# Two attention hops on a graph: the near gather from three bf16 parts of the table instead of fp32, with other buffers moved into the table's memory

## What is computed

```
h = concat(emb[head], emb[tail]) @ fc_w.T + fc_b
e = leaky_relu(sum(h * rel_e, -1), 0.2)
w = segment_softmax(e, head)
agg = segment_sum(emb[tail] * w[:, None], head) + emb
emb = agg / max(norm(agg), 1e-12)
```

## Time and profile before

| | |
|---|---|
| median of 3 runs | 5189.71 us |
| the profiled execution | 5187.74 us |
| its span, first to last instruction | 5185.9 us |
| TensorE clock granted, mean of the span | 0.899 |
| instructions | 194597 |
| busy share: PE, PEld, DVE, ACT, POOL | 79%, 64%, 71%, 45%, 62% |

### The profile page before, as it was taken

How to read it: one execution, slowest core, us unless ns; L and a number is a source line. 1 busy time by engine, 2 the same in 40 slices (tenths; PEclk the granted TensorE clock), 3 DMA queues, 4 the chain that set the end, 5 groups by cost and what they waited for, 6 DMA issues and landing times. The chain is left out here.

```text
span 5185.9 us, 194597 instructions
## 1 busy us (share of the span) xinstructions
PE 4116.0 (79%) x51067; PEld 3327.7 (64%) x51068; DVE 3702.4 (71%) x11149; ACT 2328.1 (45%) x5659; POOL 3224.1 (62%) x3241
## 2 busy tenths in 40 slices
PE   2666666629999999999759999999999478888874
PEld 0001111119999999999759999999999356666664
DVE  7988488647777777777767777777777545555555
ACT  6201000016666666666536666666666112222221
POOL 0055677637777777777447777777777067777774
PEclk7667888759999999999879999999999589899897
DMA  7999999936556666566356565665566133333332
GB/s 269 421 410 411 419 419 417 410 86 165 157 160 159 160 159 160 159 159 158 78 142 162 156 161 159 162 158 160 157 161 153 21 68 68 69 69 69 69 69 47
DMA packets 502232, 935.41 MB, mean 180 GB/s; under 512 B 153045, under 2 KB 301966, under 8 KB 452978
## 3 DMA queue, kind: packets, MB, share of 16 engines
q1 hardware_dynamic: 397729, 759.23, 45.5%
q0 software_dynamic: 103328, 174.55, 14.2%
q10 hardware_dynamic: 1072, 0.31, 0.0%
HBM read 917.50 MB, written 14.15 MB: 180 GB/s over the span
## 5 line engine op out<-in xcount | busy, mean ns | idle before, releaser
L1525 POOL DMA_INDIRECT rows<-tab_d,stage_idx x2040 | 1963.0, 962 | 922.7 <-issue 380.1
L1593 PE MATMUL ps_g<-rows,prob 128*128 128x65 f32 x6528 | 867.0, 276 | 188.8 <-issue 148.1
L1593 PEld LDWEIGHTS ps_g<-rows,prob 128*128 128x128 f32 x6528 | 795.7, 192 | 270.3 <-issue 270.3
L1908 POOL DMA_INDIRECT tab<-y_d,stage_src x768 | 732.6, 954 | 369.0 <-issue 174.9
L1619 ACT ACTIVATE prob<-ps_p 128x512 f32<-128x512 f32 x816 | 487.4, 597 | 873.9 <-PE ps_p L1572 774.7
L596 PE MATMUL ps_gate<-ring,h_sb 128*1 128x512 f32 x3072 | 551.7, 802 | 387.9 <-DMA ring<-w_ih 192.5
L1555 PE MATMUL ps_t<-tab,hot_near 128*128 x5712 | 834.0, 286 | 13.3 <-DVE hot_near L1709 11.5
L1555 PEld LDWEIGHTS ps_t<-tab,hot_near 128*128 128x128 f32 x5712 | 707.0, 193 | 23.3 <-issue 13.9
L1682 DVE CUSTOM_DVE_ANT_0 masked<-lower,ps_s,m_old 128x512 f32<-128x512 bf16 x816 | 609.8, 747 | 138.9 <-DVE x_sum L1673 99.1
L533 POOL DMA_INDIRECT rec_d<-arena,row_all x294 | 346.4, 1178 | 468.2 <-PE ps_gate L596 415.9
L2000 DVE TENSOR_SCALAR to_node<-wins_list,row_all 128x384 bf16<-128x384 bf16 x864 | 289.9, 340 | 461.8 <-PE ps_all L1949 439.6
(11 more groups left out here) (477 smaller groups left out, 6535.6 us busy)
## 6 DMA issues: line engine op xcount, KB each, us to landing
arena<-lo_d SPq DMA_DIRECT2D x816, 256.0 KB
ring<-w_ih SPq DMA_DIRECT2D x192, 1024.0 KB
ring<-w_hh SPq DMA_DIRECT2D x192, 1024.0 KB
arena<-code_d SPq DMA_DIRECT2D x408, 160.0 KB
rows<-tab_d,stage_idx POOLq DMA_INDIRECT x2040
arena<-list_lo_d SPq DMA_DIRECT2D x216, 128.0 KB
arena<-code_d SPq DMA_DIRECT2D x408, 64.0 KB
tab<-y_d,stage_src POOLq DMA_INDIRECT x768
```

The lines of the kernel that those rows point to most:

```text
L1525: pool.indirect_dma_start(out=rows[:, h * 4 + g, k, :], out_offset=None, in_=tab_d[hop], in_offset=bass.IndirectOffsetOnAxis(ap=stage_idx[ ...
L1593: mm = pe.matmul(ps_g[:, p, 0:C + 1], lhsT=prob[:, p, k * P:(k + 1) * P], rhs=rows[:, u, k, 0:C + 1], start=(k == 0), stop=(k == KT - 1))
L1908: pool.indirect_dma_start(out=rows[:, g, k].rearrange("p j c -> p (j c)"), out_offset=None, in_=y_d, in_offset=bass.IndirectOffsetOnAxis(a ...
```

## The change

1. A second table `tab_bf` [128, 51, 3, 115] bf16 holds three bf16 parts of each row, one and tail score, whose sum is the f32 value exactly. `gather` multiplies with it: `hot_near` becomes bf16, and each block has three bf16 matmuls (parts j = 0, 1, 2) instead of one fp32 matmul.
2. `tab_bf` has 51 blocks instead of 75. The first block of the late tile is set to 0 where it would lie behind them, by arithmetic in registers of PE's queue.
3. A class `Parts` makes the parts: twelve casts on ACT and eight subtractions on POOL a hop, in halves of the blocks, with semaphores between the two. Before hop 0 they stand in the second block of preparation (POOL after its indirect DMAs, ACT before the sigmoid), before hop 1 some of the casts between the steps of the projection, the rest behind it.
4. `rows`, `masked`, `prob_t`, `prob`, `lower` and `hot_near` lie in the memory of `tab` during a hop. So the rows of hop 0 come from `x0` in the `finish` before hop 1 and from the sum of the three parts in the last one, which has two more additions on DVE for each half.
5. The transposes of the projection take 65 rows instead of 128. In the last stage `y` lies in `tab_bf`'s memory.

```diff
@@ Tables
-                self.project = Project(ph, hop, tab, p12, P, 2 * R, rows_rdy, turned, ps)
+                self.project = Project(ph, hop, tab, p12, C + 1, 2 * R, rows_rdy, turned, ps)
@@ new tile and class
+        tab_all = sb("tab_all", [P, NBT * 3 * TW + NBT * 3 * TW % 2], BF16)
+        tab_bf = tab_all[:, 0:NBT * 3 * TW].rearrange("p (b j w) -> p b j w", b=NBT, j=3)
+        class Parts:
+            CASTS = ((0, 0), (1, 0), (0, 1), (1, 1), (0, 2), (1, 2), (2, 0), (3, 0), (2, 1), (3, 1), (2, 2), (3, 2))
+            RESTS = ((0, 0), (1, 0), (0, 1), (1, 1), (2, 0), (3, 0), (2, 1), (3, 1))
...
+            def cast(self, act, n):
+                unit, j = self.CASTS[n]
+                if j == 0:
+                    if self.ready:
+                        self.ready(act, unit)
+                    src = self.whole(unit)
+                else:
+                    act.wait_ge(self.rest_rdy, self.rests_before + self.RESTS.index((unit, j - 1)) + 1)
+                    src = self.rest(unit)
+                act.activation(self.part(unit, j), src, ACT.Copy).then_inc(self.part_rdy, 1)
+            def pool(self, pool):
+                for unit, j in self.RESTS:
+                    pool.wait_ge(self.part_rdy, self.parts_before + self.CASTS.index((unit, j)) + 1)
+                    pool.tensor_tensor(self.rest(unit), self.rest(unit) if j else self.whole(unit), self.part(unit, j),
+                                       ALU.subtract).then_inc(self.rest_rdy, 1)
@@ second block of preparation, gpsimd
-                pool.memset(tab[:, NB:NBW, :], 0.0).then_inc(const_rdy, 1)
+                pool.memset(tab_bf[:, NB:NBT], 0.0).then_inc(const_rdy, 1)
+                pool.memset(tab_bf[:, 0:NB, 0, ONE:ONE + 1], 1.0).then_inc(const_rdy, 1)
+                pool.memset(tab_bf[:, 0:NB, 1:3, ONE:ONE + 1], 0.0).then_inc(const_rdy, 1)
@@ finish
-            step(dve.tensor_tensor(emb, emb, sq, ALU.add))
+            if old is None:
+                step(dve.tensor_tensor(emb, tab_bf[:, lo:hi, 0, 0:C], tab_bf[:, lo:hi, 1, 0:C], ALU.add))
+                step(dve.tensor_tensor(emb, emb, tab_bf[:, lo:hi, 2, 0:C], ALU.add))
+            step(dve.tensor_tensor(emb, emb if old is None else old[:, lo:hi], sq, ALU.add))
@@ before hop 1, scalar
-                                tables.scalar(act, {3: lambda: norm_root(act, 2, *halves[1])})
+                                tables.scalar(act, {3: lambda: norm_root(act, 2, *halves[1]), 5: lambda: parts.cast(act, 0),
+                                                    **{8 + n: lambda n=n: parts.cast(act, 1 + n) for n in range(5)}})
+                                for n in range(6, len(parts.CASTS)):
+                                    parts.cast(act, n)
@@ a hop's buffers
-                rows = sbh("rows", [P, 8, KT, W])
+                in_tab = tab[:].rearrange("p b w -> p (b w)")
+                rows = in_tab[:, 0:8 * KT * W].rearrange("p (u k w) -> p u k w", u=8, k=KT)
...
-                hot_near = sbh("hot_near", [P, 2, GW + GW_B, P])
+                hot_near = in_tab[:, at:at + (GW + GW_B) * P].bitcast(BF16).rearrange("p (i b e) -> p i b e", i=2, b=GW + GW_B)
@@ gather
-                                parts = [(0, 0, GW, first + w * GW)]
+                                tiles = [(0, 0, GW, first + w * GW)]
                                 if near_tiles(u) == 2:
-                                    parts.append((1, GW, GW_B, first_late + w * GW_B))
+                                    late = pe.snap(first_late + w * GW_B)
+                                    tiles.append((1, GW, GW_B, late * (1 - ((late + OVER) >> 6))))
...
                                     for b in range(width):
-                                        mm = pe.matmul(ps_t[:, k * TW:(k + 1) * TW], lhsT=hot_near[:, p, at0 + b, :],
-                                                       rhs=tab[:, ds(at + b, 1), 0:TW].rearrange("p a c -> p (a c)"),
-                                                       start=False, stop=(b == width - 1), skip_group_check=True)
+                                        for j in range(3):
+                                            mm = pe.matmul(ps_t[:, k * TW:(k + 1) * TW], lhsT=hot_near[:, p, at0 + b, :],
+                                                           rhs=tab_bf[:, ds(at + b, 1), j, :].rearrange("p a c -> p (a c)"),
+                                                           start=False, stop=(j == 2), skip_group_check=True)
```

More of the change, by code:

```diff
@@ L183, in gnn_kernel @@
     NBW = MAX_NEAR * GW_B
+    NBT = -(-NB // GW_B) * GW_B
+    OVER = 64 - (NBT - GW_B + 1)
+    assert 0 <= OVER and NBW - GW_B + OVER < 128
     FAR_REL = 90
@@ L1030, in gnn_kernel, with __init__, whole, part @@
         far_bias = sb("far_bias", [P, 1])
+        halves = ((0, half_cut), (half_cut, NB))
+        class Parts:
+            CASTS = ((0, 0), (1, 0), (0, 1), (1, 1), (0, 2), (1, 2), (2, 0), (3, 0), (2, 1), (3, 1), (2, 2), (3, 2))
+            RESTS = ((0, 0), (1, 0), (0, 1), (1, 1), (2, 0), (3, 0), (2, 1), (3, 1))
+            part_rdy, rest_rdy = fc_ld, piece_ld[RING - 1]
+            def __init__(self, hop, scores, ready=None):
+                self.scores, self.ready = scores, ready
+                self.parts_before = FC_BEFORE + hop * len(self.CASTS)
+                self.rests_before = PIECES_BEFORE + hop * len(self.RESTS)
+            def whole(self, unit):
+                lo, hi = halves[unit % 2]
+                return tab[:, lo:hi, 0:C] if unit < 2 else self.scores(lo, hi)
+            def part(self, unit, j):
+                lo, hi = halves[unit % 2]
+                return tab_bf[:, lo:hi, j, 0:C] if unit < 2 else tab_bf[:, lo:hi, j, SC:SC + R]
+            def rest(self, unit):
+                lo, hi = halves[unit % 2]
+                w = C if unit < 2 else R
+                at = NB * W + lo * C
+                return tab[:].rearrange("p b w -> p (b w)")[:, at:at + (hi - lo) * w].rearrange("p (b w) -> p b w", w=w)
+            def cast(self, act, n):
[13 more added lines that the diff above has]
+                                       ALU.subtract).then_inc(self.rest_rdy, 1)
+        assert NB * C <= (NBW - NB) * W
         to_turn, turned_rdy, to_store, list_ld, list_st = map(sem, ("to_turn", "turned_rdy", "to_store", "list_ld", "list_st"))
@@ L1082, in gnn_kernel @@
             rec_ld, fields_rdy, near_ld = sem2("rec_ld"), sem2("fields_rdy"), sem2("near_ld")
+            parts = Parts(0, lambda lo, hi: tab[:, lo:hi, SC:SC + R])
             block = ph.enter_context(nc.Block())
@@ L1107, in _ @@
                         in_offset=bass.IndirectOffsetOnAxis(ap=tile_at[:, c:c + 1], axis=0)).then_inc(rec_ld, 16)
-                pool.wait_ge(const_rdy, 2)
+                parts.pool(pool)
+                pool.wait_ge(const_rdy, 4)
                 pool.wait_ge(near_ld, NEAR_COLS * 16)
@@ L1272, in _ @@
                 act.activation(dis[:], dis[:], ACT.Sqrt).then_inc(sq_rdy, 1)
+                for n in range(len(parts.CASTS)):
+                    parts.cast(act, n)
                 act.wait_ge(s_rdy, 1)
@@ L1316, in gnn_kernel, with made @@
                         tables = Tables(st, hop, rows_rdy)
+                        def made(act, unit):
+                            if unit < 2:
+                                act.wait_ge(rows_rdy, unit + 1)
+                            else:
+                                act.wait_ge(tables.project.taken, len(cuts4) // 2 if unit == 2 else len(cuts4))
+                        parts = Parts(hop, lambda lo, hi: tables.a_all[:, lo:hi, R:2 * R], made)
                         def sbl1(name, shape, dt=F32):
@@ L1367, in _ @@
                                 for n, (lo, hi) in enumerate(halves):
-                                    finish(dve, link, n + 1, lo, hi)
+                                    link.mark(dve.memset(tab[:, lo:hi, ONE:ONE + 1], 1.0))
+                                    finish(dve, link, n + 1, lo, hi, x0)
                                     dve.sem_inc(rows_rdy, 1)
@@ L1425, in gnn_kernel @@
                 stage_idx = sbh("stage_idx", [P, 2, 16], I32)
-                rows = sbh("rows", [P, 8, KT, W])
+                in_tab = tab[:].rearrange("p b w -> p (b w)")
+                rows = in_tab[:, 0:8 * KT * W].rearrange("p (u k w) -> p u k w", u=8, k=KT)
+                at = 8 * KT * W
+                masked, prob_t, prob = (in_tab[:, at + j * 2 * GE:at + (j + 1) * 2 * GE].rearrange("p (i e) -> p i e", i=2)
+                                        for j in range(3))
+                at += 6 * GE
+                lower = in_tab[:, at:at + 2 * GE].bitcast(BF16).rearrange("p (i e) -> p i e", i=4)
+                at += 2 * GE
+                hot_near = in_tab[:, at:at + (GW + GW_B) * P].bitcast(BF16).rearrange("p (i b e) -> p i b e", i=2, b=GW + GW_B)
+                assert at + (GW + GW_B) * P <= NBW * W
                 heads = arena.bitcast(BF16)[:, 0:8 * sum(HEAD)].rearrange("p (b e) -> p b e", b=8)
```

(1 more changed line is left out.)

15 lines of the change are left out of this document (7 added, 8 removed).

## The result

The changed kernel takes **6033.48 us** (6027.59 to 6070.35, 4 runs) against 5189.58 for the kernel before: a ratio of **1.164** [1.160, 1.169], 844 us more. The forecast was slower, 5750 us in a range of 5490 to 5920: the direction is right, the size is 283 us short and outside the range. The profiled execution took 6036.59 us, its span is 6034.8.

What follows compares the result with a forecast made beforehand. In the hops PE's array, the path PE, ACT, PE, and DVE tie, with PE's instruction queue as fourth bound, which the added addresses lengthen. 5187.7 + 514 + 45 - 2 + 7 = 5752 us, say 5750; range 5490 to 5920.

Steps and rivals of the forecast that it cites:

- What bounds the kernel: In the hops: PE's array, the path PE, ACT, PE, and DVE tie within 0.1 us; PE's instruction queue is a fourth.
- Part 1: Gather: three bf16 matmuls a block make the array lighter if each costs under 0.075 us.
- Parts 2 and 3: Gather on PE's queue: 0.13 us for each (block, part) address, 0.25 us for the late tile's clamp; +514 us.
- Part 4: Loop ends of the hops: the 1.2 us lost at the end of each eight-group turn stays.
- Part 5: Clock in the hops: some of 102 loop ends are followed by a narrow body at 1.2 GHz; +45 us, at most 150.
- rival C: Hops: the clock falls inside every turn, not only at its ends; +861 us, about 6050 us, chance 0.08.
- Part 6: hot_near in bf16 takes less of DVE, worth up to 0.26 us a pair only if DVE were the bound; here nothing.
- Part 7: Rows, masks and probabilities in the table's memory: same instructions, 0; POOL's gathers wait for a later PE, 0.
- Part 8: Splitting before each hop, casts on ACT and subtractions on POOL: 0, bound 20 us; large memset gone: -2 us.
- Part 9: Last normalization: two more additions for each half on DVE's chain, 1.89 us each for the larger half; +7 us.
- Rivals A and B: Hops. A: addresses come free, about 5091 us, chance 0.07. B: addresses cost only 0.06 us, 5355 us, chance 0.07.

## Why the forecast was wrong, step by step

- *What bounds the kernel* (the queue, level with ACT and VectorE): right. Busy shares of all engines fell and the time rose.
- *Part 1, the array*: right. The bf16 matmul of 115 columns steps by 0.054 us at one address, under the 0.075 that part 1 asked for. The Trainium skill's figure, cited there from "TensorE: Matmul & The Clock Gate", section "Back-to-back issue gap" (81 ns a matmul with its weight load, at 128 columns), is not met at 115: the measurement decides.
- *Parts 2 and 3, addresses and clamp*: right. 15 and 6 address instructions, steps of 0.131 to 0.135 us (0.13), 4.64 us a wide body (4.65), 3.12 a narrow one (3.1), 0.21 to 0.22 us for the clamp (0.25). The pair at full clock is 7.76 us (7.75), +514 us.
- *Part 4, the turn's end stays*: nearly. The turn's last body is 5.95 - 4.64 = 1.31 us over a wide one, where it was 4.40 - 3.44 = 0.96. That is 0.35 us a turn, some 35 us.
- **Part 5, the clock, is the step that failed.** It let the clock fall only behind "some of the 102 loop ends", priced that at 45 us, 150 at most, and put nothing inside the turns. Measured are 24% of the hops' time at 1.2 GHz and 273 us. 166 of them lie where the forecast looked: not some but 97 of 102 loop ends are followed by a drop, each costs the narrow body 1.3 us (the forecast's ceiling was half of 3.06), and the wide body behind it, which the term left out, another 0.35 us on average. The other 107 us lie behind ordinary wide bodies: there 90 of 300 narrow bodies have low clock in them, as in the one that takes 4.18 us for 3.12. That is rival C's mechanism, for the smaller part of the cost. C had 0.08, on the ground that "the rest of the pair, 5.5 us, is as dense as today". The wide gather had been read as thin (C: "thin gather of 2 us in each wide body"), and a thin stretch of 3.4 us followed by a drop was on show in the earlier trace rows; the forecast used it for the loop ends only. The range left C out whole. That C's price, 6050 us, comes within 17 us of the result is luck: a third of the time at low clock makes 347 us beside the 514, 74 too many, and C has none of the 64 us that the turn's end, the preparations and the last normalization cost.
- *Part 6, the narrower hot_near*: right, 0 on the path, though the instruction is shorter. *Part 7*: right on the first chip.
- *Part 8, splitting at 0, at most 20 us*: the hops start 12.8 and another 9.2 us later, 22 in all (without subtractions about 32 are gained). The reason given for the bound, a late store behind ACT's casts, is not what happened; VectorE was held by GpSimd's subtractions, which the part had priced and taken as hidden. The memset's -2 us is inside this figure.
- *Part 9, +7 us*: +6.6 us after hop 1, in these two rows of four (1.89 us each, as forecast).

```profile
4922.12 1.89 DVE L1346 TENSOR_TENSOR tab<-tab_all 128x1664 f32<-128x1664 bf16 x1
4924.04 1.89 DVE L1347 TENSOR_TENSOR tab<-tab,tab_all 128x1664 f32<-128x1664 f32 x1
```

By its own terms: forecast 514 + 45 - 2 + 7 = 564; found 514 + 35 + 273 + 22 + 7 = 851, for a measured 849 between the spans. Rivals A and B are out by the steps of 0.131 to 0.135 us. The clock's 273 us are counted in the first chip's own trace. What brings the drops is shown on other chips (fillers -74 us, fewer columns +38, the low clock gone where fillers stand); how much of it a filler would give back on the first chip isn't measured.

No variant beats the kernel before. The nearest, one matmul of 345 columns a block, equals it on two chips (1.001 and 1.003) and would still have to add its parts, for which the sums of two tiles (690 columns) have no room in one row of 512.

## What to carry to other kernels

Before a narrower type replaces one wide pass by several, count the addresses, not the columns: a matmul at a register's offset cost 0.13 us of PE's queue, its 115 columns 0.054 us. Where such a stretch becomes the bound, look what follows it: each thin stretch in a loop body is a candidate for a drop of the clock, and the drop is paid in the dense work behind it. Where a standstill at the loop's end comes on top, price nearly every end at a drop (97 of 102 here), not some of them. A side computation handed to GpSimd is free only while VectorE does nothing that needs the ports they share.

## What the runs showed that was not expected

- Useless work paid: five idle matmuls in each wide body took 74 us off, and taking two thirds of the gather's columns away added 38 us, both through the granted clock (0.83 to 0.88, 0.86 to 0.77).
- The same kernel took 5190 us on one chip and 6450 to 6540 on three others, with waits that the first chip's trace does not have and a last stage of 1528 us for 1158; on the second of them, where both ran, the change costs 5%, not 16%.
- A two-input operation on GpSimd held a VectorE instruction from 0.55 to 7.21 us.
